# Another order of the stages in part two of a landmark-attention and feed-forward kernel

## The reference

```python
q_l = q.reshape(B, H, M, denom, HS).sum(axis=-2) / denom
k_l = k.reshape(B, H, M, denom, HS).sum(axis=-2) / denom
s1 = softmax(einsum('bhld,bhmd->bhlm', q, k_l))
s2 = softmax(einsum('bhmd,bhnd->bhmn', q_l, k_l))
s3 = softmax(einsum('bhmd,bhld->bhml', q_l, k))
out = s1 @ (moore_penrose_pinv(s2, 6) @ (s3 @ v))
out = out.transpose(0, 2, 1, 3).reshape(B, L, A) @ Wo + bo
# ffn: xr, xk are mixes of a token and the one ahead of it
r = sigmoid(xr @ W_r.T);  k_act = square(relu(xk @ W_k.T));  ffn = r * (k_act @ W_v.T)
x = x + layernorm(attn(layernorm(x)));  x = x + layernorm(ffn(layernorm(x)))
```

## Time and profile before

| | us |
|---|---|
| median of 3 executions (lowest, highest) | 2005.51 (2004.91, 2010.79) |
| the profiled execution, its own time | 2001.4 |
| span of the profiled execution | 1999.7 |
| PE busy | 1623.2 (81%) |
| DVE busy | 1460.2 (73%) |
| ACT busy | 983.9 (49%) |
| POOL busy | 253.8 (13%) |

### The profile page before, as it was taken

How to read it: one execution, slowest core, us unless ns; L and a number is a source line. 1 busy time by engine, 2 the same in 40 slices (tenths; PEclk the granted TensorE clock), 3 DMA queues, 4 the chain that set the end, 5 groups by cost and what they waited for, 6 DMA issues and landing times. The chain is left out here.

```text
span 1999.7 us, 50433 instructions
## 1 busy us (share of the span) xinstructions
PE 1623.2 (81%) x21132; PEld 1120.6 (56%) x21132; DVE 1460.2 (73%) x3164; ACT 983.9 (49%) x1599; POOL 253.8 (13%) x134
## 2 busy tenths in 40 slices
PE   2758868588576898898998999899898988888786
PEld 1547756477534556655654655564565565556554
DVE  8487793877865489579768957966876895796465
ACT  1147821488223554654554455465456546544442
POOL 4000000000200011111101211111120111111122
PEclk9969989699878899999999999999999999999888
DMA  5230001000122113131211213222122231311100
GB/s 165 75 106 3 4 23 53 2 3 3 44 61 68 34 43 76 42 85 50 60 57 50 75 31 85 56 62 63 46 72 56 53 77 42 85 40 45 33 32 32
DMA packets 125697, 104.60 MB, mean 52 GB/s; under 512 B 30368, under 2 KB 123424, under 8 KB 125472
## 3 DMA queue, kind: packets, MB, share of 16 engines
q1 hardware_dynamic: 124320, 99.29, 18.0%
q10 hardware_dynamic: 1152, 2.10, 0.3%
HBM read 56.23 MB, written 19.92 MB: 38 GB/s over the span
## 5 line engine op out<-in xcount | busy, mean ns | idle before, releaser
L760 ACT ACTIVATE p<-wide 128x1024 f32<-128x1024 f32 x128 | 124.0, 1021 | 118.6 <-PE wide L1461 117.9
L1521 PE MATMUL bank<-wrT,xrT 128*128 128x256 f32 x512 | 144.7, 445 | 46.1 <-ACT vv L726 36.2
L1042 DVE TENSOR_REDUCE m<-wide 128x16 f16<-128x1024 f32 x128 | 150.4, 1216 | 40.8 <-PE wide L1345 40.3
L737 ACT ACTIVATE e<-wide 128x1024 f32<-128x1024 f32 x128 | 124.4, 1021 | 83.6 <-PE wide L1378 72.3
L1521 PEld LDWEIGHTS bank<-wrT,xrT 128*128 128x128 f32 x512 | 113.0, 226 | 72.8 <-issue 40.0
L1034 DVE TENSOR_REDUCE m<-wide 128x2 f32<-128x1024 f32 x128 | 149.8, 1212 | 2.9 <-PE wide L1325 2.9
L610 POOL TENSOR_TENSOR ob<-ob,xm 128x1024 f32<-128x1024 f32 x32 | 77.0, 2405 | 472.9 <-DVE ob L273 472.9
L1501 PE MATMUL bank<-wo,oT 128*128 128x256 f32 x512 | 120.9, 390 | 6.2 <-DVE xT L1002 3.6
L1531 PE MATMUL acc<-xkT,wkT 128*128 128x512 f32 x256 | 120.0, 613 | 7.1 <-DVE xkT L1115 7.1
L1543 PE MATMUL bank<-wvT,ka 128*128 128x256 f32 x512 | 117.6, 383 | 1.3 <-ACT x2T L785 0.8
L594 POOL TENSOR_TENSOR xm<-yy,xres 128x1024 f32<-128x1024 f32 x32 | 76.1, 2379 | 325.9 <-issue 265.5
(11 more groups left out here) (283 smaller groups left out, 3866.8 us busy)
## 6 DMA issues: line engine op xcount, KB each, us to landing
x1in<-in_L_attn_x SPq DMA_DIRECT2D x8, 2048.0 KB, 14.0
xin<-in_L_attn_x SPq DMA_DIRECT2D x32, 512.0 KB, 4.3
k_stack<-kh SPq DMA_DIRECT2D x256, 64.0 KB, 2.0
xres<-in_L_attn_x SPq DMA_DIRECT2D x32, 512.0 KB, 4.1
out<-ob SPq DMA_DIRECT2D x32, 512.0 KB, 5.2
k_stack<-kl SPq DMA_DIRECT2D x128, 64.0 KB, 2.0
q_stack<-landmarks SPq DMA_DIRECT2D x192, 4.0 KB, 1.7
inverse<-X ACTq DMA_DIRECT2D x8, 256.0 KB, 2.2
```

Source lines behind the costliest of these rows:

```text
L737: sc.activation(e3[w][:, :], wide[w][:, :], ACT.Exp).then_inc(wide_drained[w], 1)
L760: sc.activation(p1[:, 2 * j:2 * j + 2, :], wide[w][:, :].rearrange("p (a n) -> p a n", a=2), ACT.Exp).then_inc(wide_drained[w], 1)
L1042: v.tensor_reduce(m1[:, tiles, 2 * w:2 * w + 2, :].rearrange("p t q x -> p q t x"), wide[w][:, :].rearrange("p (q t x m) -> p q t x m", q= ...
L1521: ins = mm(bank[j][:, t * A:(t + 1) * A], xrT[:, k, tok], wrT[:, k, :], start=(k == 0), stop=(k == KB - 1))
```

## The change

Only the three tables are replaced. The stages, their instructions and their waits are the same; the functions stand seven lines lower in the file. `PRO` shrinks from 34 entries to 11, `LAST` grows from 133 to 193, `BODY` keeps its 139. A turn of `BODY` used to begin at C1 of chunk 2 and to end with GR and GB of the same batch's chunk 1. Now it begins at AK of chunk 0 and ends with E1 of chunk 1, so that O, T, G and most of E and H of a batch stand in the next turn.

```diff
-        PRO = [("X", 0), ("XA", 0), ("X", 1), ("XA", 1), ("R", 0), ("X", 2), ("X", 3), ("Q", 0), ("AK", 0), ("XA", 2),
...
-        BODY = [("C1", 2, 0), ("R", 3, 0), ("GK", 1, -1), ("C2", 2, 0), ("O", 3, -1), ("B2", 2, 0), ("T", 2, -1),
...
+        PRO = [("X", 0), ("XA", 0), ("X", 1), ("XA", 1), ("K", 0), ("R", 0), ("Q", 0), ("AQ", 0), ("X", 2), ("X", 3),
+               ("XA", 2)]
+        BODY = [("AK", 0, 0), ("C1", 0, 0), ("KC", 0, 0), ("AV", 0, 0), ("R", 1, 0), ("E2", 1, -1), ("O", 0, -1),
...
```

More of the change, by code:

```diff
@@ L319, in sandwich @@
         fin_out = [sem(f"fin_out{i}") for i in range(2)]
-        PRO = [("X", 0), ("XA", 0), ("X", 1), ("XA", 1), ("R", 0), ("X", 2), ("X", 3), ("Q", 0), ("AK", 0), ("XA", 2),
[3 rows of a table removed]
-        BODY = [("C1", 2, 0), ("R", 3, 0), ("GK", 1, -1), ("C2", 2, 0), ("O", 3, -1), ("B2", 2, 0), ("T", 2, -1),
[19 rows of a table removed]
-        LAST = [("C1", 2, 0), ("R", 3, 0), ("GK", 1, -1), ("C2", 2, 0), ("GO", 0, -1), ("O", 3, -1), ("KC", 2, 0),
[18 rows of a table removed]
+        PRO = [("X", 0), ("XA", 0), ("X", 1), ("XA", 1), ("K", 0), ("R", 0), ("Q", 0), ("AQ", 0), ("X", 2), ("X", 3),
+               ("XA", 2)]
+        BODY = [("AK", 0, 0), ("C1", 0, 0), ("KC", 0, 0), ("AV", 0, 0), ("R", 1, 0), ("E2", 1, -1), ("O", 0, -1),
[19 rows of a table added]
+        LAST = [("AV", 0, 0), ("E2", 1, -1), ("O", 0, -1), ("D", 2, -1), ("OA", 0, -1), ("C1", 0, 0), ("H", 1, -1),
[27 rows of a table added]
         USES = {"R": (1, 0, 0), "AQ": (1, 0, 0), "AK": (0, 0, 1), "AV": (1, 0, 0), "B1": (0, 1, 0), "B2": (0, 1, 0),
```

## The result

| | before | after |
|---|---|---|
| median of 20 runs each, us | 2003.3 | 2013.75 |
| span of the profiled execution | 1999.7 | 2013.9 |
| PE busy / idle in the fourth turn, M to M | 155.4 / 15.6 | 156.6 / 18.5 |
| PE busy / idle in a turn, mean of five | 153.9 / 16.0 | 157.0 / 18.5 |
| DVE busy in a turn, mean of five | 129.4 | 134.2 |

A forecast was written before the change was run, and what follows sets the result against it. PE was taken as the bound, waiting on DVE's queue. Its waits sum to 20.8 us idle a turn against 15.6, +5.2; six turns give 31, head and tail 0, so 2033 us, range 1980 to 2057.

The forecast's parts named there:

- place 1: E1 of chunk 2 needs both wide buffers cleared of B2 by DVE: PE waits 2.95 us a turn.
- 2, GR of chunk 0: GR waits 4.3 us for R's first bank, cleared behind TA and H; 2.3 without TA's collision with POOL's residual.
- 3, B1 of chunk 2: B1's second buffer must be cleared of C1 of chunk 2, now last in DVE's row: wait 4.2 us.
- 4, M to G2 of chunk 2: FS 0 waits for ACT, R for XA, FV 1 for DVE's FV 0: 4.1 us, against 1.9 before.
- 5, end of FS and FV, W, V, H: Waits at the last FS and FV, W, V and H: 3.5 us a turn, against 3.15 before.
- kA_bd's reload: Rival at C1 of chunk 0: reload late behind SP's stores, 3 us a turn, 2050 us; chance 0.1.
- the clock I take as equal: Two drops of 1.6 to 1.8 at GR become two, behind GR of chunk 0 and B1 of chunk 2; no change.
- PRO and the first M ... 0: Head of the kernel: both orders issue the same work for four chunks, so 0 us, bounds ±5.
- the last 178 us ... 0: Tail: LAST has 5 us more work beside FS and FV, then the same chain: 0, bounds ±8.
- six turns at +5.2: Six turns of BODY have the full pattern, each with 5.2 us more idle PE: 31 us.
- The faster case: Rival: old waits go and new ones are 9.2 us a turn smaller than walked, giving 1977 us; chance 0.22.
- The case of more clock drops: Rival: waits at E1 of chunk 2 and from M to G2 each drop the clock by 1.7: 2052 us; chance 0.1.

The follow-up runs named there:

- the experiment on `PRO`: Kernel before, with only PRO replaced by the order its stages have in the kernel after: ratio 0.9983 to the kernel before.
- The experiment on the old `LAST`: Kernel before, with TA of chunk 0 moved ahead of OA of chunk 1 in LAST: ratio 0.9978 to the kernel before.
- third: Kernel after, with GA of chunk 0 and N of chunk 2 moved behind C1 of chunk 2 in BODY: ratio 0.9951 to the kernel before.
- fourth: Kernel after, with XA of chunk 0 ahead of GA of chunk 1 and XA of chunk 1 behind FV 1 in BODY: ratio 1.0015 to before.
- `LAST` experiment: Kernel after, with TA of chunk 0 moved behind OA of chunk 1 in LAST for the last batch: ratio 1.0073 to the kernel before.
- first experiment: Kernel after, with TA of chunk 0 moved ahead of OA of chunk 1 in BODY: ratio 0.996 to the kernel before.
- second experiment: Kernel after, with OA of chunk 1 moved behind R of chunk 2 in BODY: ratio 0.9886 to the kernel before.
- three and four edits: Kernel after with the second, third and fourth edits together: 1949.8 us; then also OA, N and NA of chunk 0 moved later in BODY: 1947.8 us.
- the last experiment: Kernel before, with XA of chunk 3 of the next batch moved behind its R of chunk 2 in BODY: ratio 0.9847, 1973.0 us.

## Why the prediction was right and wrong

**Right: the mechanism and the places.** All five places wait, for the producer that was named, except that ACT is named for D and AQ beside place 1. In us a turn, measured in the turn shown:

| place | forecast | measured |
|---|---|---|
| 1, E1 of chunk 2 (with D, AQ) | 2.95 | 2.3 (0.77 + 0.39 + 1.14) |
| 2, GR of chunk 0 | 4.3 | 4.6 |
| 3, B1 of chunk 2 | 4.2 | 3.3 |
| 4, M to G2 of chunk 2 | 4.1 | 4.3 (0.26 + 1.20 + 0.22 + 1.87 + 0.76) |
| 5, end of FS and FV, W, V, H | 3.5 | 2.4 |
| small, elsewhere | 2.85 - 1.1 | 1.6 (the rest of 18.5) |

GR of chunk 1, FV 5 and FV 6 wait for nothing, and kA_bd's reload holds nothing: those statements stand. Places 1 and 3 are each 0.65 to 0.9 smaller. The walk let DVE work without a pause and PE at full clock; PE's own stages and small waits on the way give DVE a little more time than that. These six come to 20.8 forecast and 18.5 measured. Place 4 was right in sum and not in its parts: both XA met POOL, not only the first. The turn of the kernel before that was read had 15.6 of idle PE, and the mean of the five is 16.0, so idle PE rose by 2.4 a turn where the sum had 5.2.

**Wrong: "the clock I take as equal".** It cost 3.1 us of busy PE a turn. GR of chunk 0 took 5.41 before in four of seven turns only, and 3.72 in the other three. Now it takes 5.1 to 6.4 in every turn, and R, GK, FV 1 and FS 2 run slow behind places 3 and 4, where I had counted one drop for each of places 2 and 3. This error has the opposite sign and hides the other. A full turn came out at +5.5 (27.5 over five) where the sum had +5.2, and that they agree is luck: 2.4 of idle and 3.1 of clock, not 5.2 of idle and no clock.

**Wrong: the ends, "PRO and the first M ... 0", "the last 178 us ... 0", and six turns at +5.2.** This is the step that made the forecast miss. Five turns lie between the second M and the seventh, and they gave +27.5 where five times 5.2 is 26. All the rest of the kernel was forecast at +5 (the sixth turn) and came out at -13.3. The first M came 5.4 earlier, just beyond the bound of 5, and the first turn was 1.4 shorter. From the seventh M to the end it was 6.5 shorter. The sum's sixth turn is split over these two ends: its places 1 to 3 lie between the first M and the second, its places 4 and 5 behind the seventh. They wait there as forecast, and the stretches were shorter even so. I had argued from equal work: both orders issue the same stages for four chunks. But in the head DVE and PE take turns in waiting for each other's B and C, and in the experiment on `PRO` both did more from 552 to 600: DVE 36.3 us of work instead of 31.5, and PE 269 matmuls instead of 250. That experiment alone gives 5.9 of M's start. The eight traces with the new head have the first M at 621.6 to 625.3, the three with the old one at 627.0 to 629.4, so this is no accident of one execution. For the tail I had the evidence in the earlier trace rows and used it only to price place 2. It also said that the old tail pays 3.25 and 3.0 there, and the new `LAST` has TA ahead of OA for the last batch, so it does not. The experiment on the old `LAST` gives 2.4 of the 6.5 for it; what makes up the rest, and the 1.4 of the first turn, is open. I had not walked `LAST` at all. The waits of places 2 and 3 do not occur in it.

**The sum as it came out.** +27.5 for five turns, -5.4, -1.4 and -6.5 make +14.2 between the two traces. The ratio says 11.4, the medians 10.5. The rest is which executions were profiled: the one before ran 1.9 below its median, the one after 1.9 above.

**The rivals.** The faster case needed places to be 9.2 smaller a turn; they were 2.3 smaller. Its argument that half clock lets DVE catch up is the direction in which places 1 and 3 erred, at under half its price. The collision with POOL, which it had left out, is shown: it costs 2.0 of wait at place 2 (4.62, and 2.62 without it). The case of more clock drops, 3.4 a turn from places 1 and 4, was nearly right in size (3.1), and half right in place: FV 1 and FS 2 behind place 4 run slow, nothing behind place 1 does.

## What to carry to other kernels

An order is worth what its worst few rows cost: here one or two entries of `BODY` moved the time by 0.4 to 1.7% each, in four of five cases more than the 0.57% of the whole exchange of tables, and the gains of three places added up. So price the steady turn by walking the queues, but walk the head and the tail too, since equal work there does not mean equal time, and count how often the full turn really occurs; and when the traces show a slow instruction as evidence for a new place, ask at once whether the old place has gone. Read more than one turn, too: the turn read before the forecast had a clock drop that three of seven turns lack. Before an order is judged as worse, its few longest waits should be looked at: this one is 0.6% slower as written, and 2.6% faster with four small moves. The old order gained 1.5% by a single one, and it was not mended further, so which of the two orders could be the better one is not shown.

## What the runs showed of the hardware that was not expected

- The length of the wait ahead of GR of chunk 0 goes with what GR itself takes. Behind waits of 4.5 to 4.6 it took 5.1 to 6.7 us in all 24 turns (kernel after, third, fourth and `LAST` experiment). Behind 2.5 to 2.6 it took 3.69 in four turns and 5.38 in two (first experiment). Behind 1.3 it took 3.69 in all 18 (second experiment, three and four edits). In the kernel before, the pause ahead of C, just in front of GR of chunk 0, is 1.36 or 1.37 in all seven turns, and GR took 5.41 in four of them and 3.72 in three. So the last wait alone does not settle it, and no run here separates what else does. Taking waits away paid more than their length: the second experiment took 3.3 of wait ahead of GR out of each of six turns and some 34 us out of the whole.
- Two operations of POOL back to back (2.61 and 1.89 us) held two XA of DVE for 6.59 instead of 2.7 us, while POOL's own residual lost at most 0.4 (2.74 against 2.35). In these overlaps DVE pays nearly the whole price.
- Turns of one kernel with almost the same waits differ: in the trace of the last experiment one of 167.7 us has PE busy for 153.7 at clock 0.97, and the next, of 164.4, for 151.2 at 0.99; the waits differ by less than 1 us in all.
